# One ring of three PSUM banks in an attention and routing stage, the diagonal masked last, row sums by a column of ones

## The reference, cut to what matters

```python
x = x + L0_conv(gn(x))          # not touched by the change
t = to_tokens(x)                # 16 images of 1024 tokens, 128 channels
t = t + attn(ln(t)); t = t + ffn(ln(t))

# attn(E)
W = einsum('bqd,bkd->bqk', Q, K) / sqrt(D)
M = where(W == 0, 0, tril)
x_max = max(W, axis=-1)         # over all keys, not only the causal ones
x_exp = exp(W - x_max) * M
A = x_exp / (sum(x_exp, axis=-1) + 1e-9)
return einsum('bqk,bkd->bqd', A, V)

# ffn(x): router logits, softmax, top 2 of 8 experts, gates of the two,
# out = sum over the two of gate * w2(silu(w1 x) * (w3 x))
```

## Time and profile before

| | us |
|---|---|
| median of 3 runs | 2365.29 (2364.75 to 2367.83) |
| profiled execution, its time | 2363.08 |
| profiled execution, its span | 2361.3 |
| TensorE busy | 2031.8 |
| VectorE busy | 1444.6 |
| GpSimd busy | 1006.0 |
| ScalarE busy | 997.0 |

### The profile page before, as it was taken

How to read it: one execution, slowest core, us unless ns; L and a number is a source line. 1 busy time by engine, 2 the same in 40 slices (tenths; PEclk the granted TensorE clock), 3 DMA queues, 4 the chain that set the end, 5 groups by cost and what they waited for, 6 DMA issues and landing times. The chain is left out here.

```text
span 2361.3 us, 46450 instructions
## 1 busy us (share of the span) xinstructions
PE 2031.8 (86%) x11636; PEld 1462.9 (62%) x11637; DVE 1444.6 (61%) x4059; ACT 997.0 (42%) x2116; POOL 1006.0 (43%) x1345
## 2 busy tenths in 40 slices
PE   5999999999999974988888878886099999999998
PEld 4555555555555532655555555554098888888887
DVE  4666666666666642787677777876444444444443
ACT  1455554545555531433333333332044444444443
POOL 2121221212122111145544544555467777777776
PEclk7999999999999996999999999998599999999999
DMA  5222222222222212011111111111134444444443
GB/s 198 61 68 59 69 60 63 66 58 68 57 68 62 63 66 86 19 38 59 46 41 57 44 45 45 53 38 47 55 51 57 56 56 57 57 58 57 56 56 47
DMA packets 175904, 139.58 MB, mean 59 GB/s; under 512 B 33694, under 2 KB 163142, under 8 KB 175558
## 3 DMA queue, kind: packets, MB, share of 16 engines
q0 software_dynamic: 55808, 52.50, 13.9%
q1 hardware_dynamic: 120005, 86.09, 13.1%
HBM read 31.47 MB, written 46.71 MB: 33 GB/s over the span
## 5 line engine op out<-in xcount | busy, mean ns | idle before, releaser
L1457 POOL DMA_INDIRECT out<-f_y,f_rows x272 | 424.1, 1559 | 45.4 <-POOL f_waited L1455 39.8
L395 DVE TENSOR_REDUCE neg_max<-s_bank 128x2 f32<-128x512 f32 x512 | 329.9, 686 | 172.0 <-PE s_bank L600 171.5
L1531 DVE SCALAR_TENSOR_TENSOR f_hidden<-f_silu,f_rows,f_h_bank 128x341 f32<-128x341 f32 x272 | 155.2, 571 | 259.7 <-ACT f_silu L1494 206.9
L489 ACT ACTIVATE probsT<-st_bank 128x512 f32<-128x512 f32 x512 | 277.4, 593 | 36.6 <-PE st_bank L618 35.4
L975 POOL DMA_INDIRECT routed<-a_rows,a_target_idx x256 | 252.2, 985 | 74.5 <-issue 74.5
L1305 PE MATMUL a_score_bank<-a_eT,a_gT 128*128 128x512 f32 x512 | 253.2, 619 | 19.6 <-DVE a_causal_probs L1043 11.0
L630 PE MATMUL o_bank<-probsT,v_ones 128*64 128x512 f32 x1024 | 249.4, 608 | 0.0
L287 POOL TENSOR_TENSOR waited<-nothing 128x1 int32<-128x1 int32 x64 | 12.1, 190 | 547.5 <-DVE q_low L384 547.4
L1582 PE MATMUL f_y_bank<-w,f_hiddenT 114*128 (+1 forms) x1632 | 233.1, 278 | 0.9 <-DVE f_y L1522 0.6
L1494 ACT ACTIVATE f_silu<-f_h_bank 128x341 f32<-128x341 f32 x272 | 124.2, 457 | 211.1 <-PE f_h_bank L1566 164.3
L1582 PEld LDWEIGHTS f_y_bank<-w,f_hiddenT 114*128 114x128 f32 (+1 forms) x1632 | 203.2, 191 | 12.2 <-issue 11.4
(11 more groups left out here) (197 smaller groups left out, 3647.6 us busy)
## 6 DMA issues: line engine op xcount, KB each, us to landing
q_stack<-q_high SPq DMA_DIRECT2D x512, 64.0 KB, 2.4
f_rows<-routed SPq DMA_DIRECT2D x272, 66.0 KB
q_stack<-q_low POOLq DMA_DIRECT2D x256, 64.0 KB, 2.6
a_staged<-X SPq DMA_DIRECT2D x16, 512.0 KB, 3.0
out<-X SPq DMA_DIRECT2D x16, 512.0 KB
X<-in_x SPq DMA_DIRECT2D x1, 6144.0 KB, 22.1
out<-f_y,f_rows POOLq DMA_INDIRECT x272
q_stack<-max_rows SPq DMA_DIRECT2D x256, 4.0 KB
```

Of the source, the lines that this page charges most:

```text
L395: dve.tensor_reduce(neg_max[:, i % 2, CT * j:CT * (j + 1)], s_bank[h % 2][:], AX_X, ALU.max, negate=True).then_inc(max_ready, 1)
L489: act.activation(probsT[:, i % 2, c, lt, :], st_bank[lt][:], ACT.Exp).then_inc(exp_done, 1)
L1457: pool.indirect_dma_start(out=out, out_offset=bass.IndirectOffsetOnAxis(ap=rows[:, i, TOKEN:TOKEN + 1].bitcast(I32), axis=0), in_=y[:, i, ...
```

## The change

- The single bank, and the two banks of the transposed probabilities, become one ring of three banks of 512 columns, `work`. The table `USES` gives all 24 uses of an image in order: twelve for the transposes (tiles 4 to 7 in two parts), twelve for the preparations; use n has bank n modulo 3, each bank its own two semaphores.
- ScalarE's `turned` copies a part of up to four blocks from each bank of the ring, and `exps` no longer waits for the transposes of tile i - 2.
- VectorE masks after `exp_done`, in the same step as the maximum, last in the step. GpSimd multiplies the diagonal block after `masked`; only the last transpose of a tile waits for it.
- The row sum is a 129th column of the sums: `val` has a column of ones. The small addition and the reciprocal stand in `add`.
- Preparations have other steps: c at 1, v at 2 of the image itself, e at 3, g at 4, r at 5, l at 6. `choose` is cut in two, first choice at step 7, second at step 0. `targets` go to step 5, `gates` to 6.
- Scatters go from steps 3 to 7 to steps 6 and 7 and steps 0, 1 and 2 of the next period (3, 4, 4, 2, 3 of them). In a step GpSimd's order is diagonal, roots, scatters.
- The loop covers images 4 to 13; one more period stands at the end.

```diff
-SHARED = (("x0", 1, 0, 0), ("x1", 1, 0, 1), ("c", -2, 2, 0), ("e0", 1, 3, 1), ("e1", 1, 4, 0), ("g0", 1, 4, 1),
-          ("g1", 1, 5, 0), ("r0", -1, 5, 1), ("r1", -1, 6, 0), ("l", -1, 6, 1), ("v0", 1, 7, 0), ("v1", 1, 7, 1))
-KINDS = [use[0] for use in SHARED]
-
-STATS_AT, NORM_AT, TARGETS_AT, ROUTE_STATS_AT, ROUTE_NORM_AT, CHOOSE_AT = 1, 2, 3, 3, 4, 7
-SCATTERS_AT = {3: (0, 1), 4: (2, 3, 4), 5: (5, 6, 7), 6: (8, 9, 10, 11), 7: (12, 13, 14, 15)}
-SUMS = 4
+def turn_parts(j):
+
+    return 1 if j < TT // 2 else 2
+
+
+def bank_uses():
+
+    prepared = {0: (("x0", 1), ("x1", 1)), 1: (("c", -2),), 2: (("v0", 0), ("v1", 0)), 3: (("e0", 1), ("e1", 1)),
+                4: (("g0", 1), ("g1", 1)), 5: (("r0", -1), ("r1", -1)), 6: (("l", -1),), 7: ()}
+    uses = []
+    for i in range(TT):
+        j = (i - 2) % TT
+        uses += [(f"t{j}{part}", 0 if i >= 2 else -1) for part in range(turn_parts(j))]
+        uses += prepared[i]
+    return uses, prepared
+
+
+WORK_BANKS = 3
+USES, PREPARED = bank_uses()
+BANK = {kind: n % WORK_BANKS for n, (kind, _) in enumerate(USES)}
+BACK = dict(USES)
+PER_BANK = len(USES) // WORK_BANKS
+
+STATS_AT, NORM_AT, ROUTE_STATS_AT, ROUTE_NORM_AT, TARGETS_AT, GATES_AT = 1, 2, 3, 4, 5, 6
+FIRST_CHOICE_AT, SECOND_CHOICE_AT = 7, 0
+SCATTERS_AT = {6: (0, 1, 2), 7: (3, 4, 5, 6)}
+LATE_SCATTERS_AT = {0: (7, 8, 9, 10), 1: (11, 12), 2: (13, 14, 15)}
...
-        t_bank = ps("turn_bank", [P, TT, P])
-        o_bank = ps("sum_bank", [P, P])
-        shared = ps("shared_bank", [P, 512])
+        work = [ps(f"work_bank{i}", [P, 512]) for i in range(WORK_BANKS)]
+        o_bank = ps("sum_bank", [P, P + 1])
...
+                def scatters(slot, which):
+                    for n in which:
+                        t, k = n // TOP, n % TOP
+                        pool.indirect_dma_start(
+                            out=routed,
+                            out_offset=bass.IndirectOffsetOnAxis(ap=target_idx[:, slot, t, k:k + 1], axis=0),
+                            in_=rows[:, slot, t, :], in_offset=None).then_inc(scattered[slot], 16)
+
                 def period(b, slot):
                     for i in range(TT):
                         if has(b):
-                            pool.wait_ge(exp_done, b * TT + i + 1)
+                            pool.wait_ge(masked, b * TT + i + 1)
                             block_ = probs[:, i % 2, i * P:(i + 1) * P]
                             pool.tensor_tensor(block_, block_, tril[:], ALU.mult).then_inc(diag_done, 1)
                         if i == STATS_AT and has(b + 1):
                             pool.wait_ge(ve_ready, b + 2)
                             pool.tensor_tensor(ln_rs[:], ln_ve[:], minus_half[:], ALU.pow).then_inc(rs_ready, 1)
+                        if i == ROUTE_STATS_AT and has(b - 1):
+                            pool.wait_ge(rt_ve_ready, b)
+                            pool.tensor_tensor(rt_rs[:], rt_ve[:], minus_half[:], ALU.pow).then_inc(rt_rs_ready, 1)
+                        if i in LATE_SCATTERS_AT and has(b - 3):
+                            scatters(1 - slot, LATE_SCATTERS_AT[i])
...
-                def mask(b, slot, i):
+                def mask(b, i):
 
                     n = (i + 1) * P
-                    one = slice(i % SUMS, i % SUMS + 1)
-                    dve.wait_ge(diag_done, b * TT + i + 1)
+                    dve.wait_ge(exp_done, b * TT + i + 1)
                     dve.scalar_tensor_tensor(out=probs[:, i % 2, 0:n], in0=s_bank[i % 2][:, 0:n], scalar=0.0,
-                                             in1=probs[:, i % 2, 0:n], op0=ALU.not_equal, op1=ALU.mult,
-                                             accum_out=row_sum[:, one]).then_inc(masked, 1)
-                    dve.wait_ge(masked, b * TT + i + 1)
-                    dve.tensor_scalar(row_eps[:, one], row_sum[:, one], ATTN_EPS, None, ALU.add).then_inc(eps_added, 1)
-                    dve.wait_ge(eps_added, b * TT + i + 1)
-                    dve.reciprocal(row_inv[:, one], row_eps[:, one]).then_inc(inv_ready, 1)
+                                             in1=probs[:, i % 2, 0:n], op0=ALU.not_equal, op1=ALU.mult
+                                             ).then_inc(masked, 1)
 
                 def add(b, slot, i):
-                    one = slice(i % SUMS, i % SUMS + 1)
-                    dve.wait_ge(inv_ready, b * TT + i + 1)
-                    dve.wait_ge(o_full, b * TT + i + 1)
-                    dve.scalar_tensor_tensor(out=XT[:, b, i, :], in0=o_bank[:], scalar=row_inv[:, one],
+
+                    n = b * TT + i + 1
+                    dve.wait_ge(o_full, n)
+                    dve.tensor_scalar(row_eps[:], o_bank[:, P:], ATTN_EPS, None, ALU.add).then_inc(eps_added, 1)
+                    dve.wait_ge(eps_added, n)
+                    dve.reciprocal(row_inv[:], row_eps[:]).then_inc(inv_ready, 1)
+                    dve.wait_ge(inv_ready, n)
+                    dve.scalar_tensor_tensor(out=XT[:, b, i, :], in0=o_bank[:, 0:P], scalar=row_inv[:],
                                              in1=XT[:, b, i, :], op0=ALU.mult, op1=ALU.add).then_inc(added, 1)
...
-                        before_ = tile(b, slot, i - 1)
-                        if has(before_[0]):
-                            mask(*before_)
                         if has(b):
                             tile_max(b, i)
-                        summed = tile(b, slot, i - 3)
-                        if has(summed[0]):
-                            add(*summed)
-                        if i == 0 and has(b - 2):
-                            gates(b - 2, slot)
+                        if i == SECOND_CHOICE_AT and has(b - 2):
+                            second_choice(b - 2)
                         if i == STATS_AT and has(b + 1):
                             token_stats(b + 1)
                         if i == NORM_AT and has(b + 1):
                             token_norm(b + 1)
-                        if i == TARGETS_AT and has(b - 2):
-                            targets(b - 2, slot)
                         if i == ROUTE_STATS_AT and has(b - 1):
                             route_stats(b - 1)
                         if i == ROUTE_NORM_AT and has(b - 1):
                             route_norm(b - 1, 1 - slot)
-                        if i == CHOOSE_AT and has(b - 1):
-                            choose(b - 1)
+                        if i == TARGETS_AT and has(b - 2):
+                            targets(b - 2, slot)
+                        if i == GATES_AT and has(b - 2):
+                            gates(b - 2, slot)
+                        if i == FIRST_CHOICE_AT and has(b - 1):
+                            first_choice(b - 1)
+                        summed = tile(b, slot, i - 3)
+                        if has(summed[0]):
+                            add(*summed)
+                        if has(b):
+                            mask(b, i)
...
-                        if i == 0 and has(b - 2):
+                        if i == SECOND_CHOICE_AT + 1 and has(b - 2):
                             gate_exps(b - 2)
-                        outs(i, 0)
-                        turned_ = tile(b, slot, i - 2)
-                        if has(turned_[0]):
-                            turned(*turned_)
+                        image, _, j = tile(b, slot, i - 2)
+                        if has(image):
+                            turned(image, b, j, image * TT + j)
+                        prepared = [kind for kind, back in PREPARED[i] if has(b + back)]
+                        for kind in prepared[:1]:
+                            evacuate(b, slot, kind)
                         if has(b):
                             exps(b, i)
-                        outs(i, 1)
+                        for kind in prepared[1:]:
+                            evacuate(b, slot, kind)
...
-                def turn(b, slot, i):
-                    pe.wait_ge(masked, b * TT + i + 1)
-                    wait(pe, turned_out, b * TT + i)
-                    for t in range(i + 1):
-                        last = pe.transpose(t_bank[:, t, :], probs[:, i % 2, t * P:(t + 1) * P], ident[:])
-                    last.then_inc(t_full, 1)
-
-                def values(b, slot, i):
+                def turn(at, j, n):
+
+                    pe.wait_ge(masked, n + 1)
+                    for part in range(turn_parts(j)):
+                        kind = f"t{j}{part}"
+                        m = BANK[kind]
+                        wait(pe, work_free[m], use_no(at, kind))
+                        first = TT // 2 * part
+                        for t in range(first, min(j + 1, first + TT // 2)):
+                            if t == j:
+                                pe.wait_ge(diag_done, n + 1)
+                            last = pe.transpose(work[m][:, (t - first) * P:(t - first + 1) * P],
+                                                probs[:, j % 2, t * P:(t + 1) * P], ident[:])
```

(25 more changed lines are left out.)

143 lines of the change are left out of this document (72 added, 71 removed).

## The result

The changed kernel takes 2340.1 us (median of 4 runs, 2331.2 to 2341.9), the kernel before, beside it, 2365.0 (2364.0 to 2367.8): ratio 0.9885, 95% interval 0.9859 to 0.9912. It is 25 us faster; forecast were 52. The profiled execution took 2341.89 us.

The account below looks back on a forecast made before the run. No engine was full; a ring of waits bound the kernel. From the profiled 2363.1: -56.4 (period), +8 (jumps), +4 (stops), -12 (first images), -3 (image 15), +7 (tail) = 2310.7, or 2313 us with the median's 2.2 above; range 2285 to 2345.

Parts of the forecast that it names:

- the rival that TensorE stays a limit: Attention images: a third of VectorE's 6.7 us waits for sums stays; period 43.0, +29 us, 2342; chance 0.20.
- Chain of 18.2 us.: GpSimd's work from the end of tile 6's mask through eleven scatters to the token norm's inverse root, without a gap.
- Root waited for 4.4 us: VectorE waits 4.4 us per image for the token norm's root, GpSimd's 18.2 us less its own 13.8.
- Second wait 1.2: Step 3: the routing's root stands behind that tile's diagonal, which now needs the mask; VectorE waits 1.2 us per image.
- Period 40.6: Time per image in images 3 to 14: 18.2 + 21.2 + 1.2 us, 4.7 less than 45.3; twelve images, -56.4 us.
- Of the waits of VectorE for sums I let all go.: Images 3 to 14: VectorE's 79.9 us of waiting for TensorE's sums vanishes, as TensorE is ready before each add.
- Back jumps +8: Loop over image pairs: four jumps delay GpSimd's chain 2.0 us each, +8 us, range 0 to 11.
- other stops +4: Loop body: ScalarE's stops cost 0.4 us per image of ten, +4 us.
- Tail +7.: End of attention: image 13's nine queued scatters put the last routing root 19.4 us after the last mask, +7 us.
- From the ring of a tile go the 0.45 us of the diagonal.: Each tile's ring: the mask follows the exponential directly, so GpSimd's 0.45 us diagonal multiply drops out.
- GpSimd's wait does not bite: Rival: scatters fully hidden, only VectorE and two 1.2 us waits bind; period 37.4, -38 us, 2275; chance 0.08.
- the slower rival: GpSimd's queue becomes the bound with dearer scatters, 0.58 us more each: +77 us, tail +5, 2395; chance 0.06.

Follow-up runs that it names:

- third time: The changed kernel, nothing altered, run once more beside the kernel before on another occasion: 2291.3 us beside 2331.3, ratio 0.9833.
- written out: Changed kernel with its loop over pairs of images unrolled, against the kernel before: 2288.5 us, ratio 0.9829; again, ratio 0.9825, 1.6 us from the changed kernel.
- the kernel with the diagonal first: Changed kernel with GpSimd's diagonal multiply again ahead of VectorE's mask: 2245.2 us, ratio 0.9635 to the kernel before.

## Why the prediction was right, and where it was not

Faster, and within the range (2285 to 2345), but 27 us from the forecast, near the 2342 of the rival that TensorE stays a limit. Its cause is not that rival: in the longest waits TensorE's work was done. That 2340 lies in the range is in part luck, since its upper end was set to hold that rival. By the forecast's steps, changed kernel at first and on its third time:

- **Chain of 18.2 us.** Measured 17.7. Root waited for 4.4 us: 2.8, since VectorE's stretch takes 14.6 us (1478.08 to 1492.71) and not 13.8. Second wait 1.2: 1.2. Period 40.6, or 41.6 with jumps and stops: 40.65 without held signals, 43.6 with them. That 40.65 is so near 40.6 is luck too: the 40.6 stands for no jump and the full clock, and such images take 39.5, with 3.2 us of waiting for the root; four jumps and eight falls of the clock bring the average back up. The clock is a term that the sum put at nothing.
- **"Of the waits of VectorE for sums I let all go."** This is the step that failed when the change was timed: 32.1 us came back as remote. With 7.8 more of remote and 11.1 more before the maxima for scores, and less 19.8 of the wait for a_ln_rs that they hide, that is 31 of the 36 us between the occasions. Of the 11.1, one wait of 5.5 in image 13 is held like the others, its scores done; the rest may go with the lower clock. My base was read from a trace that held the same thing; the 5.10 us of the earlier trace rows were the sign. The kernel before was not profiled on an occasion without held signals, so how much of its own 79.9 us came from them stays open.
- **Back jumps +8 and other stops +4.** At the full clock a jump costs 2.1 us, as the term of 2.0 has it; with falls of the clock around it 0.4, and the whole kernel is no faster written out. Of other stops of ScalarE none is left without held signals: nothing. By the rule of the Trainium skill (Runtime: NRT & Kernel Launch, Instruction fetch mechanics) a taken branch whose target is outside the fetched window stops the engine until it is fetched; VectorE's four stops of up to 1.9 us fit that, and the 2.1 us speak for 2.0 rather than 2.7.
- **First images.** -12 forecast; up to image 3 it is 1048.42 to 1033.07, -15.
- **Image 15.** 37.5 forecast: 37.0 on the third time, 41.3 at first, with held signals in it.
- **Tail +7.** The root is 7.4 later after the mask, as forecast. But the pad transfers took 8.4 us more, and from the last mask to the first work of the third stage it is 69.8 us before, 83.2 now, +13.4. Without held signals it is 71.4. The third stage takes as long as before (658.6 and 659.0 us).
- **"From the ring of a tile go the 0.45 us of the diagonal."** Counted as a gain. The order of the masks is what the change loses by: undone, 46 us. The sum counted the chain of 18.2 rightly from the end of the mask, and priced the 1.2 us wait for a_rt_rs; what it did not ask is that the chain starts 1.7 us later only because of this order. The period of 37.4, given to the rival "GpSimd's wait does not bite", is what the kernel with the diagonal first reaches, with all sixteen scatters in their places. That its number came out is luck: GpSimd's wait did bite, until the order was turned.
- **Scatters.** 0.98 us each, no dearer; the slower rival fell.

So the sum described the changed kernel without held signals, and set it against a kernel before that was read with them. Where they are absent the gain is 40 us (2331.3 to 2291.3), where they are present 25 to 33: the change is hurt by them more, since it issues its scatters in longer rows at the turn of the image. That last reason is argued, not tested; the traces add that its granted clock in images 3 to 14 is 0.94 with them, where the kernel before has 0.99 and 0.98.

## What to carry to other kernels

When an order is moved so that one engine's step waits for another's, ask not only what the ring saves but what is queued behind the new wait: here a multiply of 0.45 us behind VectorE's mask delayed eleven scatters and two roots. A queue with a due time at both ends (roots behind it, a buffer that its last transfers must free) must be cut with both in view: what was taken from one end here was lost at the other. A wait named for no engine in the trace of before is a term of its own: look what the other engines do in it before calling it a stop. And before a term of 1 or 2 us per image is read from two runs, compare images with the same granted clock: here one fall went with 1.5 us, a jump with 2.1.

## What the runs showed of the hardware

On two occasions of four VectorE waited up to 6.4 us and ScalarE up to 6.5 us, under the name remote, for results that by the trace TensorE had finished, while GpSimd issued indirect scatters, one every 1.3 us; SyncE's sixteen transfers beside the scatters took 35.6 to 44.0 us there and 17.3 else. The same kernels differ by 1.5% (before, 2331 and 2365 to 2370) to 2.1% (changed, 2291 and 2340) between such occasions, so a comparison needs both kernels on one. TensorE's granted clock fell to its lower level after stretches in which it was nearly idle (0.11 us busy of 2), and not after every one; images with one fall took 41.0 us and those without 39.5. At that level (0.51) the scores of a tile took 2.86 us, at the full clock 1.88.
